# Local-attention row maxima from 64-query by 96-key score tiles instead of 128-query by 160-key ones

## The reference, cut to what matters

```python
sim = jnp.einsum('bhwie,bhwje->bhwij', bq, bk2) * QK_SCALE   # windows of 32 queries, 64 keys
sim = jnp.where(mask, -jnp.finfo(sim.dtype).max, sim)        # keys i-32 .. i alone are seen
attn = jax.nn.softmax(sim, -1)
out = jnp.einsum('bhwij,bhwje->bhwie', attn, bv2)
```

## Time and profile before

| | us |
|---|---|
| median of 3 runs | 3442.39 |
| lowest, highest | 3433.99, 3449.18 |
| the profiled execution's own time | 3430.56 |
| its span, first to last instruction | 3428.4 |
| mean granted clock of the matrix engine | 0.939 |

### The profile page before, as it was taken

One profiled execution on the slowest core, in us unless ns is written; L12 is line 12 of the kernel. 1 busy time (PEld: TensorE's weight loads), 2 busy tenths in 40 slices (PEclk: granted clock), 3 DMA queues, 4 the chain that ended last, 5 costly groups with the idle time before them and its releaser, 6 DMA issues.

```text
span 3428.4 us, 55664 instructions
## 1 busy us (share of the span) xinstructions
PE 3294.6 (96%) x17648; PEld 2094.4 (61%) x17648; DVE 2253.3 (66%) x3692; ACT 2308.7 (67%) x3969; POOL 1170.0 (34%) x1073
## 2 busy tenths in 40 slices
PE   5999899999999999999999999999999999999997
PEld 2444466666666666666666666666666666666664
DVE  5654476676666667667667667666766766766763
ACT  2543487777767767767767767777766777766773
POOL 2000143335433336333336333245332344333330
PEclk9965799999999999999999999999999999999997
DMA  2000010011100001100011100011100011100010
GB/s 74 1 1 1 13 44 35 34 41 42 46 36 33 34 35 50 47 30 37 34 37 51 44 33 37 31 43 47 43 33 31 37 47 43 45 31 31 37 36 20
DMA packets 101641, 121.85 MB, mean 36 GB/s; under 512 B 21972, under 2 KB 50770, under 8 KB 101458
## 3 DMA queue, kind: packets, MB, share of 16 engines
q1 hardware_dynamic: 101586, 121.15, 10.1%
HBM read 19.38 MB, written 1.05 MB: 6 GB/s over the span
## 4 chain that ended last, share of the span: by engine, by line
PE 86%; ACT 6%; DVE 5%; issue 3%; DMA 0%; SPq 0%; POOL 0%; DVEq 0%; ACTq 0%; POOLq 0%
PE ring L790 14%; PE ring L812 12%; PE ring L768 5%; PE bank L829 5%; PE ring L788 5%; PE ring L766 4%; PE ring L798 4%; PE ring L778 3%; PE bank L565 3%; PE ring L565 3%; PE bank L736 2%; PE ring L736 2%; PE ring L566 2%; PE ring L567 2%; PE bank L567 2%
## 5 line engine op out<-in xcount | busy, mean ns | idle before, releaser
L506 POOL TENSOR_TENSOR sq_lo<-sq_q,sq_hi 128x512 fp32r<-128x512 f32 x192 | 244.5, 1273 | 1500.0 <-ACT sq_hi L1009 1500.0
L790 PE MATMUL ring<-fin 64*128 64x160 f32 (+1 forms) x3072 | 608.0, 318 | 0.0
L1318 DVE TENSOR_REDUCE neg_max<-ring 128x2 bf16<-128x320 f32 x768 | 357.4, 489 | 265.7 <-PE ring L768 261.7
L812 PEld LDWEIGHTS ring<-probs_t,v_sb 128*128 128x128 f32 x3072 | 468.9, 199 | 72.9 <-issue 33.1
L790 PEld LDWEIGHTS ring<-fin 64*128 64x128 f32 x3072 | 440.5, 188 | 109.6 <-issue 4.8
L812 PE MATMUL ring<-probs_t,v_sb 128*128 128x160 f32 (+1 forms) x3072 | 506.1, 310 | 0.7 <-ACT probs_t L1033 0.7
L1024 ACT ACTIVATE neg_row<-ring 1x512 bf16<-1x512 f32 x384 | 225.1, 586 | 276.5 <-PE ring L778 271.8
L1033 ACT ACTIVATE probs_t<-ring 128x320 f32<-128x320 f32 (+1 forms) x768 | 284.1, 422 | 184.3 <-PE ring L798 184.3
L515 POOL TENSOR_TENSOR rot_k<-tc_k,ts_k 128x512 f32<-128x512 f32 x192 | 259.1, 1350 | 374.4 <-issue 374.4
L1328 DVE TENSOR_TENSOR o_feat<-ring,inv_sums 64x512 f32<-64x512 f32 x384 | 263.7, 687 | 168.4 <-ACT inv_sums L1045 165.5
L515 POOL TENSOR_TENSOR rot_q<-tc_q,ts_q 128x512 f32<-128x512 f32 x192 | 245.2, 1277 | 279.6 <-DMA ts_q<-sr_q 257.6
(11 more groups left out here) (185 smaller groups left out, 6050.3 us busy)
## 6 DMA issues: line engine op xcount, KB each, us to landing
ts_q<-sr_q SPq DMA_DIRECT2D x384, 128.0 KB, 2.0
ts_k<-sr_k SPq DMA_DIRECT2D x384, 128.0 KB, 2.0
w_raw<-in_L_ffn_Wqkv SPq DMA_DIRECT2D x48, 192.0 KB, 2.7
wo_sb<-in_L_ffn_Wo SPq DMA_DIRECT2D x6, 512.0 KB, 3.8
w_raw<-in_L_ffn_W SPq DMA_DIRECT2D x6, 341.0 KB, 3.0
rot_sb<-in_rotary SPq DMA_DIRECT2D x1, 1024.0 KB
out<-x_tok SPq DMA_DIRECT2D x16, 64.0 KB, 1.6
w_sb<-in_L_ffn_W SPq DMA_DIRECT2D x6, 128.0 KB
```

Of the source, the lines that this page charges most:

```text
L506: pool.tensor_tensor(sq_lo[:, i, :], sq[i][:], sq_hi[:, i, :].bitcast(F32), ALU.subtract).then_inc(s_sql[i], 1)
L790: pe.matmul(dst[:, at:at + q], k_fin[rows, p % 2, c * P:(c + 1) * P], q_fin[rows, p % 2, c * P:c * P + q], start=False, stop=False)
L812: mm = pe.matmul(dst[:, c * P:c * P + q], v_sb[:, c, p, h * DIM_HEAD:h * DIM_HEAD + P], probs_t[:, h, c * KEYS:c * KEYS + q], start=(c == ...
L1318: dve.tensor_reduce(neg_max[:, h, 2 * b:2 * b + 2], bank[2 + 2 * h + b][:, 0:2 * KEYS].rearrange("p (c k) -> p c k", c=2), AX_X, ALU.max, ...
```

## The change

For one head all four chunks of 128 queries now lie in one PSUM bank, each 96 columns wide (`REACH` = 64 + 32). The queries are taken in halves of 64: half e of chunk c is multiplied with the 96 keys that it can see, and written to output partitions 64e to 64e+63, columns 96c to 96c+95. So a head has one mask product of 384 columns (`NEAR`), eight score products of 96 columns with 64x64 weights, and one signal to DVE; DVE has one reduction of 128x384 to four columns. The mask constant gets another layout (384 columns in place of 480). The second bank of each head is no longer used for the rounded scores.

```diff
-    seen = (j <= i) & (j >= i - WINDOW)
-    local = np.stack([np.where(seen & (j >= 0), 0.0, MASKED), np.where(seen, 0.0, MASKED),
-                      np.where(seen, 0.0, MASKED)], 1)
+    near = (np.arange(P) % HALF_P)[:, None]
+    j = np.arange(REACH)[None, :]
+    seen = (j >= near) & (j <= near + WINDOW)
+    local = np.concatenate([np.where(seen & (j >= WINDOW - HALF_P * (i // HALF_P + 2 * c)), 0.0, MASKED)
+                            for c in range(CHUNKS)], 1)
...
-                for b in range(2):
-                    dst = bank[2 + 2 * h + b]
-                    pe.matmul(dst[:, 0:2 * KEYS], eye16, local_mask[:, b * KEYS:(b + 2) * KEYS], start=True, stop=False)
-                    for c in range(2 * b, 2 * b + 2):
-                        mm = pe.matmul(dst[:, (c % 2) * KEYS:(c % 2 + 1) * KEYS], q16[rows, p % 2, c * P:(c + 1) * P],
-                                       k16[rows, p % 2, c * P:c * P + KEYS], start=False, stop=(c % 2 == 1))
-                    mm.then_inc(s_s, 1)
+                pe.matmul(bank[2 + 2 * h][:, 0:NEAR], eye16, local_mask, start=True, stop=False)
+                for c in range(CHUNKS):
+                    for e in range(2):
+                        at = HALF_P * (2 * c + e)
+                        mm = pe.matmul(bank[2 + 2 * h][HALF_P * e:HALF_P * (e + 1), c * REACH:(c + 1) * REACH],
+                                       q16[rows, p % 2, at:at + HALF_P], k16[rows, p % 2, at:at + REACH],
+                                       start=False, stop=(c == CHUNKS - 1))
+                mm.then_inc(s_s, 1)
...
-                pe.wait_ge(s_mx, 4 * n + 2 * h + 2)
+                pe.wait_ge(s_mx, 2 * n + h + 1)
...
-                for b in range(2):
-                    dve.wait_ge(s_s, 4 * n + 2 * h + b + 1)
-                    if b == 0 and not (isinstance(n, int) and n == 0):
-
-                        dve.wait_ge(s_tm, 2 * n - 1 + h)
-                    dve.tensor_reduce(neg_max[:, h, 2 * b:2 * b + 2],
-                                      bank[2 + 2 * h + b][:, 0:2 * KEYS].rearrange("p (c k) -> p c k", c=2),
-                                      AX_X, ALU.max, negate=True).then_inc(s_mx, 1)
+                dve.wait_ge(s_s, 2 * n + h + 1)
+                if not (isinstance(n, int) and n == 0):
+                    dve.wait_ge(s_tm, 2 * n - 1 + h)
+                dve.tensor_reduce(neg_max[:, h, :],
+                                  bank[2 + 2 * h][:, 0:NEAR].rearrange("p (c k) -> p c k", c=CHUNKS),
+                                  AX_X, ALU.max, negate=True).then_inc(s_mx, 1)
```

More of the change, by code:

```diff
@@ L34 @@
 KEYS = WINDOW + P
+HALF_P = P // 2
+REACH = HALF_P + WINDOW
+NEAR = CHUNKS * REACH
 FFN = int(D * 4 * 2 / 3)
@@ L72, in shape_constants @@
     i = np.arange(P)[:, None]
-    j = np.arange(KEYS)[None, :] - WINDOW
-    seen = (j <= i) & (j >= i - WINDOW)
-    local = np.stack([np.where(seen & (j >= 0), 0.0, MASKED), np.where(seen, 0.0, MASKED),
-                      np.where(seen, 0.0, MASKED)], 1)
+    near = (np.arange(P) % HALF_P)[:, None]
[3 more added lines that the diff above has]
+                            for c in range(CHUNKS)], 1)
     key, query = np.arange(P)[:, None], np.arange(KEYS)[None, :]
@@ L79, in shape_constants @@
     causal = np.where(np.arange(P)[None, :] <= i, 0.0, MASKED)
-    masks = np.concatenate([local.reshape(P, -1), turned, turned, causal, np.eye(P), causal.T], 1).astype(np.float32)
+    masks = np.concatenate([local, turned, turned, causal, np.eye(P), causal.T], 1).astype(np.float32)
     eye = np.eye(P, dtype=np.float32)
@@ L118, in build_program @@
         bank += [ctx.enter_context(nc.psum_tensor(f"bank{i}", [P, 512], F32))[:, :] for i in (6, 7)]
[L121 to L126, removed]
+        mask_sb = sb("mask_sb", [P, NEAR + 2 * KEYS + 3 * P], BF16)
+        local_mask = mask_sb[:, 0:NEAR]
+        local_mask_t = mask_sb[:, NEAR:NEAR + 2 * KEYS]
+        causal_mask = mask_sb[:, NEAR + 2 * KEYS:NEAR + 2 * KEYS + P]
+        eye16 = mask_sb[:, NEAR + 2 * KEYS + P:NEAR + 2 * KEYS + 2 * P]
+        causal_turned = mask_sb[:, NEAR + 2 * KEYS + 2 * P:NEAR + 2 * KEYS + 3 * P]
         ones16 = sb("ones16", [1, P], BF16)
@@ L191, in build_program @@
         values = sb("values", [P, NF, TOK])
-        mask_raw = gates[:].rearrange("p a t -> p (a t)")[:, 0:5 * KEYS + 3 * P]
+        mask_raw = gates[:].rearrange("p a t -> p (a t)")[:, 0:NEAR + 2 * KEYS + 3 * P]
         wkqv_sb = values[:, 0, 0:3 * P]
```

## The result

| | before | after |
|---|---|---|
| median | 3445.78 us (4 runs) | 3317.82 us (4 runs) |
| lowest, highest | 3433.99, 3459.38 | 3271.86, 3344.53 |
| ratio | | 0.9583, 95% interval 0.9477 to 0.9689 |
| span of the profiled execution | 3428.4 | 3317.1 |

What follows compares the result with a forecast made beforehand. PE was taken as the bound: 356 heads at 0.354 us less each gave 126.0 us, less 6.5 and 1.6 us lost in waits, so 118 us off 3442.4, or 3324 us, range 3285 to 3396 us.

Steps and rivals of the forecast that it cites:

- PE is the bound, and its instructions there are worth their length: Whole kernel: PE, busy 96% of the span, is the path; an instruction removed between its waits saves its full length.
- (a): Score products: two column tiles run side by side, so a chunk's two products cost 0.040 us.
- Rivals 3 and 4: Score products: two tiles' loads one after another, 3394 us, chance 0.08; or no overlap at all, 3491 us, chance 0.05.
- (b): Score weights: a 64-column bf16 load costs 0.053 us beyond its fixed part, setting the pace; a head takes 0.613 us.
- rival 1: Score weights: narrow loads are cheap, a head takes 0.534 us, the kernel 3298 us; chance 0.15.
- Rival 2: Score products: no load under a running product of the same rows, 0.093 us per chunk, 3363 us; chance 0.12.
- DVE: Reductions: one of 557 ns replaces two of 490; the 0.42 us per head is worth nothing, and no wait appears.
- Pair 5: Pair 5 of 23 bodies: PE already waits 1.61 us for ACT's neg_row, so head 0's saving is lost, 23 heads.
- Pair 2: Pair 2 of 23 bodies: 0.28 us lost at neg_row, 6.5 us in all; 0.07 us at o_feat, 1.6 us in all.
- Rival 5: After pair 5's stall: clock stays at 0.50 through the next pair, costing 7 us per body, 3485 us; chance 0.04.
- Sum: Whole kernel: 356 heads x 0.354 = 126.0, less 6.5 and 1.6, gives 118 us saved.
- Plain pairs, ACT's 0.63 us to spare: Plain pairs: ACT's 0.39 us idle ahead of invert_sums and 0.24 us before L798 exceed the saving, so nothing is lost.

## Why the prediction was right, by its own steps

- **PE is the bound, and its instructions there are worth their length.** Right: 0.82 to 0.84 us per plain pair for two heads that are 0.41 us shorter each, and 0.22 us more per head cost 52 to 63 us. In the layers PE is busy 143 us less.
- **The mask, 0.267 us.** Right: 0.27.
- **(a) Two tiles side by side.** Right, and tested: 0.29 us against 0.27 for one full-width tile. Rivals 3 and 4 needed 0.56 and 0.84 us.
- **(b) The load of 64 columns.** Missized. I took 0.053 us beyond the fixed part; the rows say 0.027:

```profile
L772 PEld LDWEIGHTS ring<-k,q 64*64 64x64 bf16 x2872 | 83.6, 110 | 66.7 <-issue 66.7
L783 PEld LDWEIGHTS ring<-mask_sb,neg_max 128*1 128x1 bf16 x1436 | 72.8, 83 | 45.8 <-issue 5.3
```

  110 less 83 ns for 64 columns is 0.42 ns per column, half of what f32 rows gave, while 128 columns of bf16 add 12 ns. The Trainium skill, "TensorEngine Tiling (Array Packing)", Restrictions, says that column tiling turns fast weight load off. The trace agrees in direction (a narrow bf16 load takes longer than a full one, 110 ns against 95). But 0.027 us fits under a product of 0.040: loads didn't set the pace. The head came to 0.554 us, between my 0.613 and the 0.534 of rival 1, and the saving to 0.410 us, not 0.354. By my own sum that is 356 x 0.410 = 146 us.
- **Rival 2, no load under a running product of the same rows.** Wrong: its block would be 0.47 us, and it is 0.29. The rule that I weighed with it, from "TensorE: Matmul & The Clock Gate", Part 3, of the Trainium skill, isn't what this kernel shows, for full-width or for 64x64 tiles.
- **DVE.** Right: 558 ns for the reduction (557 forecast), no wait in the plain pairs. That its saving is worth nothing is shown for 0.15 of the 0.42 us, and not for pair 6.
- **Pair 5.** Right: the whole of head 0's saving became wait, 1.61 to 2.02 us.
- **Pair 2.** The place was right, the size was not. I expected 0.35 us per body lost there (0.28 and 0.07); pair 2 keeps 0.29 of 0.82, so 0.53 is lost at full clock: 12 us in 23 bodies, where I had 8. I had read the 0.07 us from the end of `neg_row` to L798 as time to spare. Of it 0.055 us is passed even when PE is waiting (in pair 5 before, and in pairs 2 and 5 after), so only 0.01 us was, and head 0 loses 0.40 us and not 0.28. The rest goes to `o_feat` at the pair's end, in front of pair 3: DVE finishes it 12.47 us into the pair in place of 12.61, so it gained 0.14 us where I had 0.28, and of the 0.166 us that I took for slack 0.057 is never free either.
- **Clock.** The sum left it out. In 11 of 22 bodies the new wait of pair 2 is followed by a dip that costs the pair 1.4 us, but fewer dips follow the layers' ends, so in the 22 middle bodies together the time at 0.50 didn't grow (180.9 us before, 177.5 after). All of the growth is in the first body (11.0 to 17.1 us) and in the last (6.8 to 23.9), whose pairs 2, 5 and 7 have more time at 0.50. The layers' time at clock 0.50 went from 198.8 to 218.5 us, some 10 us lost.
- **Rival 5, dips through the next pair.** It didn't happen: pair 6 has no time at 0.50, and pair 5's went from 129.7 to 119.5 us. Its price was too low as well, since 14 us of PE work take 14 us more at half clock, not 7. The sign that I gave for it misleads: the mean clock did fall, to 0.924 from 0.939, but 73 us of the additional time at 0.50 stand in the first stage (184 to 256 us), which the change doesn't touch, and 20 us in the layers.
- **Sum.** 146 less 12 (pair 2) less 10 (clock) is 124, and the layers became 124.7 us shorter. So the mechanism was right, but that 118 us came so near was luck: a saving sized 20 us too small, and losses 14 us too small.
- **Plain pairs, ACT's 0.63 us to spare.** Right: no waits in pairs 1, 3, 4, 6, 7 beyond those of before, and 0.20 us left: in pair 1 `neg_row` ends at 1628.87 and L803 starts at 1629.07. Less the 0.055 us that always pass, 0.15 is to spare. ACT is next in line, and DVE in pair 6.

## What to carry to other kernels

Count the changes between tile shapes on the matrix engine, products on both sides included: each costs as much as 256 columns (0.107 us at 2.4 GHz), and two fewer per head were half of this gain. A shorter bound engine arrives earlier at the waits that remain; list them before, since work saved just ahead of such a wait is worth nothing, and a short new wait can cost more in clock than in waiting. Slack is not the whole time between one engine's end and the other's start: take off what passes when the other is waiting already (here 0.055 us). When the first part of a program scatters by tens of microseconds, compare the part that the change touches, and in it the stretch at which the edit aims, since the rest of it can differ by as much as the effect.

## What the runs showed of the hardware that I had not expected

- Products given as four in one column tile and then four in the other still overlapped: 0.30 us for eight.
- Loads of bf16 weights: 83 ns for 1 column, 110 for 64 in a 64x64 tile, 95 to 100 for 128. The narrow one is the slowest.
- How long PE waits doesn't alone tell whether the granted clock falls. Waits of 0.31 to 0.35 us in front of head 0's one-row products (L803) in pair 2 were followed by a dip in 69 of 132 bodies. Waits of 0.7 us in front of pair 3's mask, behind dense projections, were followed by none, and waits of 0.25 us in front of head 1's one-row products in pair 2 by none. The last two differ from the first in place, and the last in length too; which of it decides is open.
- From the end of `neg_row` on ACT to the first product that waits for it 0.055 us pass, from the end of `o_feat` on DVE to the mask product 0.057 us.
- The first stage, the same instructions each time, lasted 405 to 454 us. Its clock and not its waits makes the difference: the shortest had clock 0.77 and PE idle for 57 us, the longest 0.65 and 52 us.
